# Queries of a latent attention: latent columns produced transposed, rotated columns token by token, three score banks

## The chip, the cores and the metric

One core of one Trainium2 chip runs the whole program. The metric is the device time of one execution in microseconds; lower is better.

## The reference

Four sequences of 512 tokens with 256 features go through two layers. Layer 0 is a multi-head latent attention (16 heads, causal) with a residual, and a mixture of 64 experts (6 per token) with a shared expert. Layer 1 is a Mamba-2 mixer and a ternary feed-forward network. The change touches the queries of the attention:

```python
q = rmsnorm(x @ w_qa, q_norm_w) @ w_qb          # (.., 192) @ (192, 16*(128+64))
q_nope, q_rope = q[..., :DN], q[..., DN:]       # DN = 128, DR = 64
kv = x @ w_kva                                   # (.., 64 + 64)
k_nope, v = split(rmsnorm(kv_c, kv_norm_w) @ w_kvb)
q_rope = q_rope * cos + rotate_half(q_rope) * sin
scores = einsum('blhd,bmhd->bhlm', q, k) * scale
attn = softmax(where(mask, scores, -1e30))
out = einsum('bhlm,bmhd->blhd', attn, v).reshape(B, L, H * DV) @ w_o
```

## The kernel before, in words

All data is float32. The part of w_kvb that makes the keys is folded into w_qb once, at the start (`prep_queries`), so that a head's query has 64 latent columns, matched with the normalised 64-wide latent itself, and 64 rotated columns: 128 in all (`QE`). Likewise the value part of w_kvb is folded into w_o (`prep_values`). The transposed keys `KT` hold 64 latent rows and 64 rotated rows for 512 tokens.

The attention goes by sequence (`b`, four) and in a sequence by groups of four heads (`g`, sixteen in all, numbered 0 to 15). A group has 16 slots: token tile `i = u // 4` (128 tokens) and head `h = u % 4`. For slot `u` TensorE makes the scores against `(i + 1) * 128` keys (L521) and adds the causal mask in bf16 (L522); VectorE takes the maximum (L853); ScalarE takes the exponential and its sum (L700); VectorE takes the reciprocal (L858) and normalises (L864); TensorE transposes the probabilities (L530) three slots later (`LAG`); VectorE copies them out (L873, L876); at three places of a group (slots 12, 16 and 20) TensorE multiplies them with the values (L547) and ScalarE copies these (L712). A group's last slots lie in the next group. PSUM has eight banks: four for scores in turn, two for transposed probabilities, one for values, and one (`QUERY`, bank 7) for making the next group's queries.

Compressed queries of 192 features lie transposed as `cq1` (128 rows) and `cq2` (64 rows, padded to 128 with zeros). Their products with the folded weights `wqe1`, `wqe2` (L480, L481) give four heads of one token tile: 128 tokens by 512 columns. ScalarE copies them to `qs` (L681). GpSimd rotates the 64 rotated columns of each head (`rope`, L964 to L968; VectorE does tiles 1 and 3 of a sequence's first group). TensorE turns each head's 128 x 128 (L486), and ScalarE copies the result to `QT` (L685). In a group with a successor in its sequence, products stand at slots 1, 3, 5, 7 and turns at 9, 11, 13, 15, written out by hand in tables (`PRODUCT_AT`, `TURN_AT`). Each engine runs its instructions in program order, and semaphores connect them. Between two sequences TensorE projects the next one, makes the mean squares, the output and the queries of the next sequence's first group in one piece (`first_queries`).

From the second sequence on, routing work of the sequence before stands in the slots too: logits and top-6 in a sequence's first group, ranks in its second, weights (VectorE) in its third and fourth; GpSimd scatters token rows to DRAM (L1198), eight of them among the turns made in the third group, sixteen in the fourth.

## Time and profile before

| | |
|---|---|
| three runs | 1368.81 us median, 1367.03 to 1376.04 |
| profiled execution: span from first to last instruction | 1372.1 us (no other time of that execution is given) |
| mean granted TensorE clock | 0.952 |
| busy over the span | TensorE 1236.2 us (90%), VectorE 801.9 (58%), ScalarE 463.7 (34%), GpSimd 376.6 (27%) |
| attention, first scores to last | about 59 to 642 us |

"Busy" counts time in which an engine works on at least one instruction. A TensorE matmul on float32 is recorded as two passes (so x2 for one matmul), and the recorded duration of a pass includes its way through the array; what it costs in a row of passes is the distance from start to start. PEld rows are weight loads, SPq rows DMA issues. Everything behind the attention (experts, Mamba, feed-forward) is not touched.

### The profile page before, as it was taken

Reading aid. Unit: us, or ns where it says so; the run is one execution under the profiler, and the core shown is the slowest. Engines: PE = TensorE matmul, PEld = TensorE weight load, DVE = VectorE, ACT = ScalarE, POOL = GpSimd, SP = SyncE. Lnnn points to the kernel's source line nnn. Section 1 sums busy time; section 2 is a strip of 40 time slices with the busy share of each in tenths; the row PEclk is TensorE's granted clock in tenths of the full one; section 3 lists DMA queues with packets and bytes.
Section 4 is the critical chain, followed back from the end, with each engine's and each line's share of the span. In section 5 each row is a group of like instructions: output and inputs, shape, how many; then the busy total and the mean of one; then the engine's idle time right before and its main releaser. Section 6 shows DMA issues by size and latency. Waiting matters only on the chain.

```text
span 1372.1 us, 19483 instructions
## 1 busy us (share of the span) xinstructions
PE 1236.2 (90%) x6005; PEld 767.3 (56%) x6005; DVE 801.9 (58%) x2226; ACT 463.7 (34%) x1057; POOL 376.6 (27%) x464
## 2 busy tenths in 40 slices
PE   6999999989999899988959999997585987999988
PEld 3566566555555466556536777775244545555454
DVE  6377767786578667784513434334665673685431
ACT  2455435442455335442201111111331612625310
POOL 1242023451425413351340000113564261311200
PEclk9799999999999999999979999999777998999999
DMA  9999999999800100010336888884212021000000
GB/s 320 413 419 420 420 421 420 420 420 418 334 1 32 62 1 1 8 58 30 107 103 191 274 263 269 270 278 138 67 43 62 1 70 39 12 12 16 0 16 16
DMA packets 89422, 235.48 MB, mean 172 GB/s; under 512 B 12768, under 2 KB 23680, under 8 KB 89088
## 3 DMA queue, kind: packets, MB, share of 16 engines
q1 hardware_dynamic: 70912, 192.54, 37.9%
q0 software_dynamic: 9216, 25.18, 5.8%
q10 hardware_dynamic: 9216, 16.78, 3.2%
q8 instruction: 42, 0.69, 0.2%
q14 instruction: 36, 0.29, 0.1%
HBM read 66.70 MB, written 167.77 MB: 171 GB/s over the span
## 4 chain that ended last, share of the span: by engine, by line
PE 72%; DVE 15%; issue 4%; another core or an unknown queue 3%; ACT 2%; SPq 2%; DMA 1%; POOL 1%; ACTq 0%; DVEq 0%; POOLq 0%
PE bank L521 6%; PE bank L547 5%; PE bank L480 4%; PE bank L609 4%; PE bank L530 4%; PE bank L481 4%; PE bank L1327 4%; PE bank L1349 3%; PE bank L1588 3%; PE bank L1594 3%; DVE negmax L853 3%; PE bank L1605 3%; DVE r L864 2%; PE bank L1639 2%
## 5 line engine op out<-in xcount | busy, mean ns | idle before, releaser
L700 ACT ACTIVATE r<-bank,negmax 128x128 f32<-128x128 f32 (+3 forms) x256 | 134.9, 527 | 173.7 <-DVE negmax L853 163.5
L521 PE MATMUL bank<-r 128*128 128x512 f32 (+3 forms) x512 | 184.2, 443 | 0.0
L853 DVE TENSOR_REDUCE negmax<-bank 128x1 f32<-128x128 f32 (+3 forms) x256 | 124.1, 485 | 55.9 <-PE bank L522 53.0
L530 PE MATMUL bank<-tables,r 128*128 128x128 f32 x640 | 117.7, 284 | 19.8 <-DVE r L864 18.6
L964 POOL TENSOR_TENSOR r<-r,tables 128x256 f32<-128x256 f32 x56 | 42.0, 749 | 331.7 <-ACT r L681 331.6
L1198 POOL DMA_INDIRECT sent<-r,slots x96 | 93.9, 978 | 113.0 <-ACT r L700 49.1
L530 PEld LDWEIGHTS bank<-tables,r 128*128 128x128 f32 x640 | 75.2, 145 | 74.6 <-issue 35.6
L1436 DVE COPY r<-bank 128x512 f32<-128x512 f32 x64 | 41.2, 685 | 116.3 <-PE bank L1358 75.3
L864 DVE TENSOR_SCALAR r<-r,rrow 128x128 f32<-128x128 f32 (+3 forms) x256 | 103.8, 406 | 0.3
L521 PEld LDWEIGHTS bank<-r 128*128 128x128 f32 x512 | 77.8, 191 | 23.6 <-issue 18.4
L1214 POOL DMA_INDIRECT r<-sent,slots x16 | 15.2, 950 | 223.3 <-DMA sent<-r 219.6
L480 PE MATMUL bank<-r 128*128 128x512 f32 x128 | 70.7, 634 | 3.6 <-DVE x L808 1.5
L1550 POOL TENSOR_TENSOR r<-tables,r 128x1024 f32<-128x1024 f32 x16 | 31.2, 1960 | 153.6 <-DVE r L1969 123.6
L873 DVE COPY late<-bank 128x256 f32<-128x256 f32 (+1 forms) x128 | 60.4, 472 | 16.5 <-PE bank L530 16.5
L481 PE MATMUL bank<-r 128*128 128x512 f32 x128 | 66.6, 602 | 0.0
L1394 ACT ACTIVATE r<-bank 128x512 f32<-128x512 f32 x32 | 19.1, 597 | 137.1 <-PE bank L1327 125.0
L1327 PE MATMUL bank<-r 128*128 128x256 f32 x256 | 62.4, 388 | 0.0
L1349 PE MATMUL bank<-r 128*128 128x256 f32 x256 | 61.3, 382 | 0.0
L609 PE MATMUL bank<-spent,r 128*128 128x256 f32 x256 | 57.9, 383 | 0.5 <-ACT r L712 0.5
L522 PE MATMUL bank<-futureb,identb 128*128 128x128 bf16 x256 | 56.1, 219 | 0.0
L609 PEld LDWEIGHTS bank<-spent,r 128*128 128x128 f32 x256 | 47.8, 190 | 11.8 <-issue 4.6
L1349 PEld LDWEIGHTS bank<-r 128*128 128x128 f32 x256 | 48.0, 190 | 8.9 <-issue 2.7
(276 smaller groups left out, 2404.4 us busy)
## 6 DMA issues: line engine op xcount, KB each, us to landing
sent<-gath SPq DMA_DIRECT2D x8, 16384.0 KB, 88.1
r<-waT_dram SPq DMA_DIRECT2D x64, 304.0 KB, 3.1
r<-sent SPq DMA_DIRECT2D x64, 256.0 KB
sent<-r ACTq DMA_DIRECT2D x64, 256.0 KB
w2buf<-wcT_dram SPq DMA_DIRECT2D x64, 48.0 KB, 3.5
r<-w_o_dram SPq DMA_DIRECT2D x1, 2048.0 KB, 11.2
sent<-gath SPq DMA_DIRECT2D x2, 1024.0 KB, 56.7
out_dram<-x SPq DMA_DIRECT2D x4, 512.0 KB, 2.9
```

The lines of the kernel that those rows point to most:

```text
L480: nc.tensor.matmul(bank[at][:], cq1[:, i * P:(i + 1) * P], w1, start=True, stop=False)
L481: nc.tensor.matmul(bank[at][:], cq2[:, i * P:(i + 1) * P], w2, start=False, stop=True)\
L521: nc.tensor.matmul(at[:, 0:n], QT[g % 2][:, h, i * P:(i + 1) * P], KT[:, 0:n], start=True, stop=False)
L530: last = nc.tensor.transpose(bank[TRANS[u % 2]][:, j * P:(j + 1) * P], prob[:, u % 4, j * P:(j + 1) * P], ident)
L547: last = nc.tensor.matmul(bank[VALUE][KVL * half:KVL * (half + 1), c:c + 2 * P], V[:, j, :], p[:, 2 * half:2 * half + 2, :].rearrange("p h ...
L609: last = nc.tensor.matmul(bank[4 + i % 2][:, 0:DIM], OT[:, c, i * P:(i + 1) * P], wvo[:, c, :], start=(c == 0), stop=(c == HEADS // 2 - 1))
L700: nc.scalar.activation(prob[:, u % 4, 0:(i + 1) * P], bank[SCORE[u % 4]][:, 0:(i + 1) * P], ACT.Exp, bias=negmax[:, u:u + 1], scale=1.0, a ...
L853: nc.vector.tensor_reduce(negmax[:, u:u + 1], bank[SCORE[u % 4]][:, 0:(i + 1) * P], axis=AX.X, op=ALU.max, negate=True).then_inc(A["max"], 1)
L864: nc.vector.tensor_scalar(p, p, rrow[:, u:u + 1], None, ALU.mult).then_inc(A["norm"], 1)
L1198: nc.gpsimd.indirect_dma_start(sent[:, :], bass.IndirectOffsetOnAxis(ap=slots[:, t, k:k + 1], axis=0), xn1[:, n // TOPK, :], None).then_in ...
L1327: last = nc.tensor.matmul(bank[2][:, t * ROWS:(t + 1) * ROWS], wb[:, 2 * q + t, k * EI:k * EI + EA], tokens(q, t, k), start=(k == 0), stop ...
L1349: nc.tensor.matmul(to[t][:, half * DIM:(half + 1) * DIM], hid_a[:, q % 2, c:c + P], wb[:, 2 * q + t, KC * EI:KC * EI + DIM], start=(half = ...
```

## The change

Latent columns are now produced already transposed: folded weights of two heads (128 columns) are the stationary operand and the 512 tokens of the compressed query move, so the result is `QT`'s latent rows. Only rotated columns are still made token by token, 256 instead of 512 per tile. The 64-row remainders stand twice, in rows 0 to 63 and 64 to 127, and two of them are issued one behind the other into two banks. Scores have three banks; the next group's queries have two (3 and 7).

```diff
-        wqe1, e = carve(r2, 0, (HEADS, QE))
-        wqe2, e = carve(r2, e, (HEADS, QE))
+        wl1, e = carve(r2, 0, (HEADS, KVL))
+        wl2, e = carve(r2, e, (GROUPS, P))
+        wr1, e = carve(r2, e, (HEADS, DR))
+        wr2, e = carve(r2, e, (HEADS, DR))
...
-            load(sp, "tables", wqe1[:, :, KVL:QE], a["w_qr"][0:P])
-            load(sp, "tables", wqe2[0:QL2, :, KVL:QE], a["w_qr"][P:QL])
+            load(sp, "tables", wr1, a["w_qr"][0:P])
+            load(sp, "tables", wr2[0:QL2], a["w_qr"][P:QL])
+            load(sp, "tables", wr2[QL2:P], a["w_qr"][P:QL])
...
-        VO_BANKS = (4, 5, 0, 1)
+        VO_BANKS = (0, 1, 2, 3)
...
+            pe.wait_ge(A["v"], 1)
...
-                for dst, b, n in ((wqe1, 4, P), (wqe2[0:QL2], 6, QL2)):
...
+                nc.scalar.copy(wl1[:, 8 * m:8 * m + 8, :], bank[4 + m][:].rearrange("p (h c) -> p h c", h=8))\
+                    .then_inc(prep_out, 1)
+            nc.scalar.copy(wl2, bank[6][:].rearrange("p (g c) -> p g c", g=GROUPS)).then_inc(prep_out, 1)
...
-        SCORE, TRANS, VALUE, QUERY = (0, 1, 2, 3), (4, 5), 6, 7
-        PRODUCT_AT = {1: 0, 3: 1, 5: 2, 7: 3}
-        TURN_AT = {9: 0, 11: 1, 13: 2, 15: 3}
+        SCORE, TRANS, VALUE, QUERY = (0, 1, 2), (4, 5), 6, (3, 7)
+        QSTEPS = TB + 2
+        ROPES_AT = {1: 0, 4: 1}
+        LATENTS_AT = 7
+        TURN_AT = {11: 0, 14: 1}
...
+            def rope_product(g, half, at):
+
+                heads_ = slice(g % GROUPS * HG, (g % GROUPS + 1) * HG)
+                for t in range(2):
+                    i = 2 * half + t
+                    nc.tensor.matmul(bank[at[t]][:, 0:HG * DR], cq1[:, i * P:(i + 1) * P],
+                                     wr1[:, heads_, :].rearrange("p h c -> p (h c)"), start=True, stop=False)
+                for t in range(2):
+                    i, r = 2 * half + t, slice(QL2 * t, QL2 * (t + 1))
+                    nc.tensor.matmul(bank[at[t]][:, 0:HG * DR], cq2[r, i * P:(i + 1) * P],
+                                     wr2[r, heads_, :].rearrange("p h c -> p (h c)"), start=False, stop=True)\
+                        .then_inc(A["q"], 1)
+
+            def latent_product(g, at):
+
                 hg = g % GROUPS
...
+                for p in range(2):
+                    h = hg * HG + 2 * p
+                    nc.tensor.matmul(bank[at[p]][:], wl1[:, h:h + 2, :].rearrange("p h c -> p (h c)"), cq1,
+                                     start=True, stop=False)
+                for c in range(0, SEQ, 2 * P):
+                    for p in range(2):
+                        r = slice(QL2 * p, QL2 * (p + 1))
+                        last = nc.tensor.matmul(bank[at[p]][:, c:c + 2 * P], wl2[r, hg, :], cq2[r, c:c + 2 * P],
+                                                start=False, stop=c + 2 * P == SEQ)
+                last.then_inc(A["q"], 1)
+
+            def rope_transposes(half, at):
+                for p in range(2):
+                    for t in range(2):
+                        last = nc.tensor.transpose(bank[at][:, (2 * p + t) * P:(2 * p + t + 1) * P],
+                                                   qs[:, 2 * half + t, p * P:(p + 1) * P], ident)
                 last.then_inc(A["qt"], 1)
...
             def first_queries(b):
                 g = GROUPS * b
...
+                pe.wait_ge(A["cq"], 3 * b + 3)
+                rope_product(g, 0, (6, 7))
+                rope_product(g, 1, (4, 5))
                 if b == 0:
                     prep_values(pe)
...
+                pe.wait_ge(A["qs"], QSTEPS * g + 2)
+                latent_product(g, (6, 7))
+                pe.wait_ge(A["qs"], QSTEPS * g + TB)
+                for half in range(2):
+                    turned(g, 2 * half)
+                    turned(g, 2 * half + 1)
+                    rope_transposes(half, 4 + half)
...
-                need(pe, A["exp"], NU * g + u - 3)
...
+                need(pe, A["exp"], NU * g + u - len(SCORE) + 1)
...
-            pe.wait_ge(prep_out, 8)
+            pe.wait_ge(prep_out, 3 + len(VO_BANKS))
...
+            def ql_copy(g, p, at):
+                act.wait_ge(A["q"], (TB + 1) * (g + 1))
+                for m in range(2):
+                    last = nc.scalar.copy(QT[g % 2][0:KVL, 2 * p + m, :], bank[at][KVL * m:KVL * (m + 1), :])
+                last.then_inc(A["qs"], 1)
+
+            def qt_copy(g, half, at):
+                act.wait_ge(A["qt"], 2 * g + half + 1)
+                for m in range(2):
+                    last = nc.scalar.copy(pairs(QT[g % 2])[KVL:QE, :, m, half * 2 * P:(half + 1) * 2 * P],
+                                          bank[at][DR * m:DR * (m + 1), :].rearrange("p (a l) -> p a l", a=2))
+                last.then_inc(A["qte"], 1)
 
             def first_queries(b):
...
+                g = GROUPS * b
+                for i, at in enumerate((6, 7, 4, 5)):
+                    q_copy(g, i, at)
+                for p, at in enumerate((6, 7)):
+                    ql_copy(g, p, at)
+                for half, at in enumerate((4, 5)):
+                    qt_copy(g, half, at)
                 if b == 0:
                     prep_values_out(act)
...
+                    if at in ROPES_AT:
+                        for t in range(2):
+                            q_copy(g + 1, 2 * ROPES_AT[at] + t, QUERY[t])
+                    if at - LATENTS_AT in (1, 2):
+                        ql_copy(g + 1, at - LATENTS_AT - 1, QUERY[at - LATENTS_AT - 1])
+                    if at in TURN_AT:
+                        qt_copy(g + 1, TURN_AT[at], QUERY[TURN_AT[at]])
...
+                    for r in (0, QL2):
+                        nc.vector.scalar_tensor_tensor(out=cq2[r:r + QL2, :], in0=bank[1][0:QL2, :], scalar=qn2[:],
+                                                       in1=rq[0:QL2, :], op0=ALU.mult, op1=ALU.mult)\
+                            .then_inc(A["cq"], 1)
...
-                        if b and hg == GROUPS - 1:
-                            if i == 0:
+                        if b and hg == GROUPS - 1 and i % 2:
+                            if i == 1:
                                 send_ready(pool, b - 1)
-                            send(b - 1, 2 * i)
-                            send(b - 1, 2 * i + 1)
+                            for m in range(4):
+                                send(b - 1, 2 * (i - 1) + m)
```

The order on TensorE in slots 5 to 9 of group 1, where the next group's queries are made: before, the last products (L480, L481) and the first turn (L486); L521 and L522 are scores and mask, L530 transposed probabilities.

```order
L480 MATMUL bank<-r 128x512
L481 MATMUL bank<-r 128x512
L530 MATMUL bank<-tables,r 128x128
L521 MATMUL bank<-r 128x256
L522 MATMUL bank<-futureb,identb 128x128
L530 MATMUL bank<-tables,r 128x128
L521 MATMUL bank<-r 128x256
L522 MATMUL bank<-futureb,identb 128x128
L480 MATMUL bank<-r 128x512
L481 MATMUL bank<-r 128x512
```

After, from slot 6 on (L554 and L555 are scores and mask, L563 transposed probabilities, L503 and L508 the latent columns' 128-row part and remainders):

```order
L554 MATMUL bank<-r 128x256
L555 MATMUL bank<-futureb,identb 128x128
L563 MATMUL bank<-tables,r 128x128
L554 MATMUL bank<-r 128x256
L555 MATMUL bank<-futureb,identb 128x128
L503 MATMUL bank<-r 128x512 x2
L508 MATMUL bank<-r 128x256 x4
L563 MATMUL bank<-tables,r 128x128 x2
L554 MATMUL bank<-r 128x384
```

The products of slots 5 and 7 became one block behind the scores of slot 7; the turns at slots 9, 11, 13, 15 became two, at 11 and 14.

The order on ScalarE in slots 8 to 12 of group 1: before (L700 exponentials, L685 turned queries, L712 values),

```order
L700 ACTIVATE r,rowsum<-bank,negmax 128x384 x2
L685 COPY r<-bank 128x4x128
L700 ACTIVATE r,rowsum<-bank,negmax 128x384 x2
L685 COPY r<-bank 128x4x128
L700 ACTIVATE r,rowsum<-bank,negmax 128x512
L712 COPY r<-bank 128x2x128 x2
```

and after (L749 exponentials, L724 latent pieces, L730 rotated pieces, L761 values):

```order
L749 ACTIVATE r,rowsum<-bank,negmax 128x384
L724 COPY r<-bank 64x512 x2
L749 ACTIVATE r,rowsum<-bank,negmax 128x384
L724 COPY r<-bank 64x512 x2
L749 ACTIVATE r,rowsum<-bank,negmax 128x384 x2
L730 COPY r<-bank 64x2x256 x2
L749 ACTIVATE r,rowsum<-bank,negmax 128x512
L761 COPY r<-bank 128x2x128 x2
```

Two copies became six, four of them ahead of the exponentials of slots 9 and 10.

The order on ScalarE before the first exponential of all: before (L401 folded query weights, L677 value rows, L681 and L685 queries, L407 folded values),

```order
L677 COPY r<-bank 128x256
L681 COPY r<-bank 128x512 x4
L407 COPY spent<-bank 128x512 x4
L685 COPY r<-bank 128x4x128 x4
L700 ACT_TABLE_LOAD
```

and after (L404 and L406 folded query weights, L712 value rows, L716, L724 and L730 queries, L411 folded values):

```order
L404 COPY r<-bank 128x512 x2
L406 COPY r<-bank 128x512
L712 COPY r<-bank 128x256
L716 COPY r<-bank 128x256 x4
L724 COPY r<-bank 64x512 x4
L730 COPY r<-bank 64x2x256 x4
L411 COPY spent<-bank 128x512 x4
L749 ACT_TABLE_LOAD
```

The copies of the folded values moved from ahead of the turned queries to behind them.

## Rows read from the trace of the kernel before

**Rows 1.** Groups 1, 3, 6: stretch, length, busy PE, PEld, DVE, ACT, POOL; clock; DMA.
```profile
84.10:112.30 28.20, 28.20 (x162) 17.22 (x160) 19.78 (x66) 15.52 (x45) 9.49 (x16) 1.00 1.02 420
140.50:160.00 19.50, 19.09 (x119) 11.37 (x115) 17.12 (x62) 10.67 (x35) 0.00 (x0) 1.00 1.02 419
260.60:290.20 29.60, 28.25 (x160) 16.91 (x158) 24.32 (x92) 14.85 (x44) 17.66 (x24) 1.00 1.03 420
```
**Rows 2.** The same view: third and fourth quarter of group 1, fourth of group 4.
```profile
99.60:104.60 5.00, 5.00 (x32) 3.32 (x30) 5.00 (x17) 3.26 (x10) 2.25 (x4) 1.00 1.02 419
104.60:112.30 7.70, 7.70 (x52) 4.88 (x52) 6.39 (x18) 4.80 (x13) 0.00 (x0) 1.00 1.03 422
221.10:228.70 7.60, 7.04 (x46) 4.23 (x44) 7.44 (x26) 4.31 (x12) 0.00 (x0) 1.00 1.03 421
```
**Rows 3.** Chain of waits in group 1, one product; timeline of TensorE, one turn.
```profile
85.62 0.91 PE bank L480 x2
86.54 0.86 PE bank L481 x2
...
79.00 0.61 PE L486 MATMUL bank<-tables,r 128*128 128x128 f32 x4
79.44 0.27 PE L530 MATMUL bank<-tables,r 128*128 128x128 f32 x1
```
**Rows 4.** Timeline of TensorE: start us, duration; half-height forms and their neighbours.
```profile
741.48 1.13 PE L1358 MATMUL bank<-w2buf,r 48*128 48x256 f32 x8
742.54 0.66 PE L1312 MATMUL bank<-tables,r 128*128 128x128 f32 x4
...
23.21 1.02 PE L460 MATMUL bank<-r,ones 128*128 128x512 f32 x2
24.16 1.12 PE L461 MATMUL bank<-r,ones 64*128 64x512 f32 x2
25.22 1.09 PE L346 MATMUL bank<-tables,late 128*128 128x128 f32 x8
```
**Rows 5.** Groups by form, ScalarE: busy us, mean ns | idle before, releaser.
```profile
L681 ACT COPY r<-bank 128x512 f32<-128x512 f32 x64 | 37.4, 585 | 40.6 <-PE bank L481 40.1 <-issue 0.5
L712 ACT COPY r<-bank 128x256 f32<-128x256 f32 x64 | 22.1, 372 | 38.0 <-PE bank L547 27.2 <-remote 8.9 <-issue 2.0
L664 ACT ACTIVATE r<-bank 64x512 f32<-64x512 f32 x8 | 4.7, 588 | 7.3 <-PE bank L452 7.3
```
**Rows 6.** Timeline of the start, up to the first scores.
```profile
40.83 2.03 ACT L401 COPY r<-bank 128x512 f32<-128x512 f32 x4 [3.30 <-PE bank L378]
42.95 2.04 PE L480 MATMUL bank<-r 128*128 128x512 f32 x2 [1.55 <-issue]
...
52.96 3.73 PE L393 MATMUL bank<-r 128*64 128x256 f32 x32
...
57.31 1.07 ACT L685 COPY r<-bank 128x512 f32<-128x512 f32 x2
...
58.99 0.39 PE L521 MATMUL bank<-r 128*128 128x128 f32 x2
```
**Rows 7.** Timeline: end of slot 6's exponential, scores of slot 9, group 3.
```profile
149.10 0.19 ACT L700 ACTIVATION_READ_ACCUMULATOR r<-bank,negmax 128x1 f32 x1
...
149.62 0.81 PE L521 MATMUL bank<-r 128*128 128x384 f32 x2
```
**Rows 8.** Busy time by stretch; the granted clock stands behind POOL.
```profile
991.00:996.20 5.20, 0.03 (x2) 0.01 (x1) 1.95 (x9) 4.07 (x8) 3.98 (x5) 0.83 0.36 107
996.20:1001.20 5.00, 5.00 (x24) 4.71 (x25) 3.03 (x6) 0.44 (x1) 4.17 (x3) 0.50 0.14 44
```
**Rows 9.** Timeline between the first and the second sequence.
```profile
181.93 0.73 DVE L792 SCALAR_TENSOR_TENSOR r<-bank,qn,r 64x512 f32<-64x512 f32 x1
...
184.37 0.32 PEld L472 LDWEIGHTS bank<-tables,r 64*128 64x128 f32 x4 [0.33 <-DVE r L796]
...
189.00 1.12 PE L480 MATMUL bank<-r 128*128 128x512 f32 x2 [0.52 <-DVE x L808]
...
199.16 0.39 PE L521 MATMUL bank<-r 128*128 128x128 f32 x2
```

More of the change, by code:

```diff
@@ L169, in build @@
         krope, e = carve(r2, e, (2, SEQ))
-        qs, e = carve(r2, e, (TB, HG * QE))
+        qs, e = carve(r2, e, (TB, HG * DR))
         qtmp, e = carve(r2, e, (2, HG * DR))
@@ L304, in loaded @@
             eng.wait_ge(loads[key], total_loads[key])
-        total_loads = {"first": 96, "x": 16, "tables": 48, "prep": 32, "w_o": 16, "ffn0": 80, "mamba": 112, "ffn1": 112}
+        total_loads = {"first": 96, "x": 16, "tables": 64, "prep": 32, "w_o": 16, "ffn0": 80, "mamba": 112, "ffn1": 112}
         class Norm:
@@ L484, in q_transpose @@
-            def q_transpose(i, at):
-                for h in range(HG):
-                    last = nc.tensor.transpose(bank[at][:, h * P:(h + 1) * P],
-                                               qs[:, i, h * QE:(h + 1) * QE], ident)
-                last.then_inc(A["qt"], 1)
+            def rope_product(g, half, at):
[9 more added lines that the diff above has]
+                        .then_inc(A["q"], 1)
@@ L490, in first_queries @@
             def first_queries(b):
                 g = GROUPS * b
-                if b == 0:
-                    pe.wait_ge(consts, 6)
-                pe.wait_ge(A["cq"], 2 * b + 2)
-                for i in range(TB):
-                    if i >= 2:
-                        pe.wait_ge(A["qs"], TB * g + i - 1)
-                    q_product(g, i, 7 - i % 2)
+                pe.wait_ge(A["cq"], 3 * b + 3)
+                rope_product(g, 0, (6, 7))
+                rope_product(g, 1, (4, 5))
@@ L559, in slot @@
                     pass
-                if not final and with_next and at in PRODUCT_AT:
-                    i = PRODUCT_AT[at]
-                    if i == 0:
-                        pe.wait_ge(A["qte"], TB * g + TB)
-                    else:
-                        pe.wait_ge(A["qs"], TB * (g + 1) + i)
-                    q_product(g + 1, i, QUERY)
-                if not final and with_next and at in TURN_AT:
-                    i = TURN_AT[at]
-                    pe.wait_ge(A["rope_p"], turns_before(g + 1, i) + 1)
-                    if i == 0:
-                        pe.wait_ge(A["qs"], TB * (g + 1) + TB)
-                    else:
-                        pe.wait_ge(A["qte"], TB * (g + 1) + i)
-                    q_transpose(i, QUERY)
+                if not final and with_next:
+                    if at in ROPES_AT:
+                        half = ROPES_AT[at]
+                        if half == 0:
+                            pe.wait_ge(A["qte"], 2 * (g + 1))
+                        else:
+                            pe.wait_ge(A["qs"], QSTEPS * (g + 1) + 2)
+                        rope_product(g + 1, half, QUERY)
+                    if at == LATENTS_AT:
+                        pe.wait_ge(A["qs"], QSTEPS * (g + 1) + TB)
+                        latent_product(g + 1, QUERY)
+                    if at in TURN_AT:
+                        half = TURN_AT[at]
+                        pe.wait_ge(A["qs"], QSTEPS * (g + 1) + TB + half + 1)
+                        turned(g + 1, 2 * half + 1)
+                        rope_transposes(half, QUERY[half])
+                if first and at == LAG:
+                    pe.wait_ge(A["qte"], 2 * (g + 1))
                 u = at - LAG
```

90 lines of the change are left out of this document (35 added, 55 removed).

## The prediction

> **What bounds the kernel now.** I read first the table of busy time by stretch, cut at the groups of the attention (a group: four heads of one sequence, 16 slots). In a group that also makes the next group's queries TensorE is busy throughout: 28.20 of 28.2 us, with VectorE at 19.78 and ScalarE at 15.52 [rows 1]. The last group of a sequence makes none and takes 19.5 us with TensorE at 19.09; so TensorE's work on queries sets the pace in the others, 12 of the 16 groups. Then I cut one group into quarters. In its third quarter (slots 8 to 11) VectorE is full as well, 5.00 of 5.0 us, in its fourth 6.39 of 7.7. With routing work added, VectorE has 7.44 of 7.6 us in the fourth quarter of the second sequence's first group, and 24.32 of 29.6 over its third group [rows 1, 2]. So time taken off TensorE in the first half of a group is time saved, and time taken off in the second half is saved only where VectorE is not full.
>
> **The change, part by part.**
>
> *Products in the first half.* Before, a tile's product is two matmuls of 512 columns, recorded as two passes each: 0.91 + 0.86 = 1.77 us [rows 3], four per group: 7.08 us. A pass over 512 columns is thus 0.43 us, over 256 columns 0.215. After, one half of the rotated columns is two 128-row matmuls of 256 columns (4 passes, 0.86 us) and two 64-row matmuls in the upper and the lower half of the array, into two banks. The trace has such a pair elsewhere: eight passes of 256 columns in the 48-row form, alternately from two halves of the array, run from 741.48 to the next form's start at 742.54, 1.06 us, where one after the other they would take 8 x 0.215 = 1.72 [rows 4]. So pairs run together (4 x 0.215 = 0.86), and 0.20 goes to the first load and the leaving of the form. Entering costs 0.09: the two 512-column passes before the 64-row form start at 23.21, the form at 24.16, and 0.95 - 0.86 = 0.09; the two passes in it, to 25.22, again cost 0.86 + 0.20 [rows 4]. A visit to the half-height form therefore costs 0.29 us beside its passes. Half of the rotated columns: 0.86 + 0.43 + 0.29 = 1.58; both: 3.16. The latent columns: 4 passes of 512 = 1.72, then 8 passes of 256 in pairs = 0.86 + 0.29: 2.87. Sum 6.03, with some 0.15 for the three entries behind the bf16 mask matmul (the 0.05 by which 0.91 exceeds 0.86): 6.18. Saved: 0.90 per group, 10.8 us over 12. I take 10.5.
>
> The Trainium skill, "TensorEngine Tiling (Array Packing)", Key Properties, says that changing the tiling mode drains TensorE; the row agrees that a change has a price. If each of the six changes in a group cost a drain, taken as the 0.17 by which a lone pass of 512 (0.60 recorded) outlasts its slot of 0.43, it would be 1.0 us a group instead of my 0.87: 1.6 us more in all. It neither carries nor changes the sum.
>
> *Turns in the second half.* Four 128-column transposes take 0.44 us (79.00 to 79.44) [rows 3]; a group has 16 before and 8 after: 0.88 us. What that is worth differs. In the first three groups of sequence 0, which have no routing and where VectorE leaves 1.3 us of the second half, I take 0.85 x 3 = 2.6; in the first groups of sequences 1 to 3, whose fourth quarter is full, 0.6 x 3 = 1.8; in the six others, where VectorE runs at 24.32 of 29.6, 0.15 x 6 = 0.9. Together 5.3; the ends are 0 and 12 x 0.88 = 10.6.
>
> *ScalarE.* Before, eight copies of 512 columns per group (0.585 each by the by-form row). After, four of 256 columns (0.372) and eight 64-partition pieces of 512 elements, for which the nearest row is 0.588 on 64 partitions: half the partitions save nothing [rows 5]. Two in a row take about 1.07 (57.31) [rows 6]. Four pieces now stand behind the exponentials of slots 8 and 9 and two behind that of slot 11, about 3.2 us of copies in a quarter that takes 5.0 and has ScalarE busy 3.26 in it, of which 1.1 goes. I followed the slots: the exponentials of slots 9 to 11 come 0.3, 0.9 and 1 us later than now, and VectorE's reciprocal waits for them; TensorE then has some 1.5 us of value products at slot 12, which hold up the scores of slot 13 anyway, and behind them the lateness ends; ScalarE has 4.80 of 7.7 us to do in that quarter. I cost it at nothing because of that cover; without it it is 1 to 2 us a group (the third rival).
>
> *Three score banks.* Scores of slot u now wait for the exponential of u-3, not u-4. In the tightest stretch of before, slots 8 to 12 of a last group, the scores of slot 9 start at 149.62, while the exponential three slots back has its accumulator read at 149.10 for 0.19, thus ends at 149.29: 0.33 us to spare [rows 7]. Transposes of u-3 already wait for a later step of the same chain. Cost 0; queued behind such a wait would be the query products and everything on TensorE, and VectorE would wait for those.
>
> *Start.* ScalarE's four copies of folded weights take 2.03 us and release the first product at 42.95; three take 1.5: -0.5 us. Cold products: 2 x 3.0 us at half clock, to 48.5. Then value folding, 3.7 [rows 6], to about 52.5, and the latent columns to 55.5, the transposes to 56.4. Now ScalarE: it stood idle for the folded values before, and copied them while they were made; after, its order is four query copies, four latent pieces, four rotated pieces and only then four copies of folded values. From 55.6: 2.1 + 2.1 + 2.1 us, so the first scores, which wait for all of them, start at about 62.0 instead of 58.99 [rows 6]: +3.0. TensorE stands idle for some 5.5 us then. In the trace a stretch of 5.2 us with TensorE busy for 0.03 is followed by 5.0 us at a granted clock of 0.50, the 1.2 GHz level [rows 8]; slots 0 to 3 would run some 3.7 us of work partly at that level: +1.8 (between 0 and 2.5). The Trainium skill, "TensorE: Matmul & The Clock Gate", HAM oscillation, says idle gaps throw the clock back; the trace agrees.
>
> *Between sequences, three times.* VectorE writes the remainder of the compressed query twice, one more 0.73 us (181.93) ahead of the key latents, for which TensorE already waits 0.33 us [rows 9]: with back-to-back overlap of 0.07 and slack of 0.3, +0.33. From the first product at 189.00 to the first scores at 199.16 it is 10.2 us. After: products and latents done at +6.1, ScalarE's latent pieces at +8.4 and rotated pieces at +9.5 and +10.6: -0.4 in effect, as the exponentials queue behind the last. TensorE's work now has idle time of some 2 us in front of the first scores and again until the first exponential; between no loss of clock and 2 us of it, I take 0.8. Sum +0.7 x 3 = 2.1.
>
> *Loads, sends.* The rotated weights arrive in rows of 4 KB rather than in pieces, so SyncE's queue moves on sooner; nothing waits for them but work behind 41 us. GpSimd's sends stand in fours behind two turns, and the turn for slot 14 is due many us later. Zero for both.
>
> **Sum.** -10.5 - 5.3 + 3.0 + 1.8 + 2.1 = -8.9 us. It is made against the profiled execution, whose span is 1372.1; the three runs have a median of 1368.8 and no launch time of the profiled one is given, so the difference is carried over: 1368.8 - 8.9 = 1360 us. The likeliest case alone spans 1353 to 1367.
>
> **Rivals.**
> - *All TensorE time is saved.* The last group's 19.5 us with VectorE at 17.12 speaks for it; the full quarters against. 12 x 1.75 = 21, less 3.0 at the start, no clock losses: 1351.
> - *VectorE or ScalarE takes the whole second half.* Then only the first half counts: -10.5 + 6.9 = -3.6: 1365.
> - *ScalarE's pieces hold up the exponentials, slower than before.* If both pairs behind slots 8 and 9 are exposed, 2.1 us x 12 = 25 us are added and the second half's gain is gone: -10.5 + 25 + 6.9 = +21.4: 1390. It makes the kernel slower by over 1% from 1.4 us a group on ((13.7 + 10.5 - 6.9)/12). For it: VectorE is full in that quarter, so nothing lost there comes back in it. Against it: the value products at slot 12.
> - *The half-height pairs run one after the other*, so that the change doesn't do what it says: 1.72 us x 12 = 20.6 more: +11.7, 1380. The pairs elsewhere [rows 4] speak against it.
>
> **How the numbers follow.** Forecast 0.48, all saved 0.20, second half lost 0.17, ScalarE exposed 0.10, no pairing 0.05. About 1% (13.7 us) is what a measurement tells from no change: faster means under 1355.1. Faster: 0.20 + 0.12 of the forecast's own range = 0.32. Slower, above 1382.5: 0.10 and 0.03 of the rest. The same: 0.55. The range 1347 to 1378 leaves out the third rival, most of the fourth, and the edge of the first.
>
> **What would show it.** Right: first halves of groups shorter by 0.9 us, second halves by 0.9 in sequence 0 and by little with routing; half-height passes in pairs a few ns apart; the first maximum near 62.5 us, with the clock at half behind it; no wait of scores on exponentials of over 0.2 us a slot. Wrong: reciprocals waiting on exponentials in slots 9 to 11 by more than 1.4 us a group; quarters three and four shorter together by over 1.5 us; half-height passes 0.2 us apart.

## The result, and the profile after

The changed kernel takes 1372.27 us (median of 14 runs, 1369.97 to 1379.49) beside 1368.61 for the kernel before (14 runs): ratio 1.0038, 95% interval 1.002 to 1.0057: slower by 0.4%, clear of noise. The forecast was 1360. Its profiled execution has a span of 1371.4 us and a mean granted clock of 0.951 (before: 1372.1 and 0.952).

The spans hide the comparison, since what follows the attention varies by some us from profile to profile (741 to 747 on this chip, whatever the kernel), and the profile of the kernel before lies above its median: elsewhere a time is 1.8 us more than its span, which would make it some 1374 us (an estimate) beside 1368.61. So I compare the attention alone, up to the last maximum of a score row: it starts at 627.4 us before, at 629.7 after. Busy time by stretch, groups 1, 3 and 6, the third and the fourth quarter of group 1, then the gap and the stretch behind it at the start and at the second sequence (columns as in [rows 1]):

```profile
89.18:116.20 27.02, 26.84 (x168) 16.63 (x164) 20.87 (x65) 16.57 (x48) 9.18 (x16) 1.00 1.02 420
143.20:162.14 18.94, 18.47 (x113) 10.95 (x109) 16.90 (x60) 10.29 (x34) 0.00 (x0) 1.00 1.02 420
262.54:291.97 29.43, 27.20 (x164) 16.17 (x162) 24.17 (x92) 16.56 (x48) 17.44 (x24) 1.00 1.02 419
103.70:109.40 5.70, 5.70 (x38) 3.60 (x38) 5.03 (x17) 5.01 (x13) 0.00 (x0) 1.00 1.03 420
109.40:116.20 6.80, 6.80 (x48) 4.16 (x44) 6.39 (x18) 5.64 (x14) 0.00 (x0) 1.00 1.02 420
56.60:62.50 5.90, 0.00 (x0) 0.00 (x0) 0.00 (x0) 5.75 (x12) 0.00 (x0) 0.94 1.02 422
62.50:69.30 6.80, 6.79 (x25) 4.92 (x26) 2.37 (x12) 3.63 (x11) 1.72 (x4) 0.55 1.03 425
200.50:202.00 1.50, 0.00 (x1) 0.02 (x1) 0.00 (x0) 1.44 (x4) 0.00 (x0) 0.92 1.02 421
202.00:205.00 3.00, 2.99 (x10) 2.31 (x10) 0.79 (x4) 2.96 (x7) 0.00 (x0) 0.50 1.02 422
```

Against [rows 1], group 1 is down from 28.20 to 27.02 and group 6 from 29.6 to 29.4. Quarters three and four of group 1 are 5.7 and 6.8 beside 5.0 and 7.7 [rows 2]: ScalarE's pieces lengthen one, and the later one gives it back (the run with small pieces, below, shows both). The last four rows are the losses: TensorE idle for 5.9 us at the start and for 1.5 us between sequences, with ScalarE at work in both, and half clock (1.2 of 2.4 GHz) behind each. Another 1.1 us of idle time stands before those 1.5 (198.73 to 199.87 us), where TensorE waits for the columns that VectorE rotates; the kernel before has gaps of 0.33 and 0.49 us in this stretch. Before, no such fall came at any of the three later sequence starts.

Timeline of the start and of the second sequence's first queries:

```profile
55.62 2.37 ACT L724 COPY r<-bank 64x512 f32<-64x512 f32 x4 [6.00 <-PE bank L508]
58.02 2.37 ACT L730 COPY r<-bank 64x512 f32<-64x512 f32 x4
60.41 2.05 ACT L411 COPY spent<-bank 128x512 f32<-128x512 f32 x4
62.51 0.79 PE L554 MATMUL bank<-r 128*128 128x128 f32 x2 [5.91 <-ACT spent L411]
...
184.09 1.51 DVE L846 SCALAR_TENSOR_TENSOR r<-bank,qn,r 64x512 f32<-64x512 f32 x2
...
187.08 0.46 PE L481 MATMUL bank<-tables,r 64*128 64x64 f32 x4 [0.49 <-DVE r L850]
...
191.71 1.13 PE L490 MATMUL bank<-r 128*128 128x256 f32 x4 [0.52 <-DVE x L862]
...
198.19 2.37 ACT L724 COPY r<-bank 64x512 f32<-64x512 f32 x4 [2.35 <-PE bank L508]
...
200.59 2.37 ACT L730 COPY r<-bank 64x512 f32<-64x512 f32 x4
202.01 0.77 PE L554 MATMUL bank<-r 128*128 128x128 f32 x2 [1.51 <-ACT r L730]
```

ScalarE's order is the forecast's, and its latent pieces begin at 55.62 as forecast; but four pieces take 2.37 us, 0.59 each, not 2.1. First product to first scores between sequences is now 10.30 us (10.16 in [rows 9]), and from there to the first maximum it is 0.98 us at half clock instead of 0.55.

TensorE's timeline in group 1, a rotated half and then the latent columns, each with what follows it:

```profile
89.87 1.08 PE L490 MATMUL bank<-r 128*128 128x256 f32 x4
90.88 0.70 PE L494 MATMUL bank<-r 64*128 64x256 f32 x4
91.52 0.66 PE L563 MATMUL bank<-tables,r 128*128 128x128 f32 x4
...
99.59 1.94 PE L503 MATMUL bank<-r 128*128 128x512 f32 x4
101.46 1.14 PE L508 MATMUL bank<-r 64*128 64x256 f32 x8
102.52 0.44 PE L563 MATMUL bank<-tables,r 128*128 128x128 f32 x2
```

A half takes 1.65 us from start to next start (forecast 1.58) and the latents 2.93 (2.87). In the single passes the two products of a pair start 6 to 7 ns apart; entering the half-height form costs about 0.09 us, leaving it 0.10, the first pair 0.10, and the second pass behind it comes 0.05 us late. With that, a group's products are 2 x 1.70 + 2.98 = 6.38 us instead of 7.08.

The distance from one group's first maximum to the next (from single records), in us after minus before: the first maximum of all +3.98; group 0 +1.07; groups 1 and 2 -1.18 each; groups 4, 8, 12 (first of a sequence) -0.72, +0.23, +0.37; groups 5, 9, 13 -0.6 each and 6, 10, 14 -0.2 each; groups 3, 7, 11 with the boundary behind them +0.60, +1.27, +0.64; group 15 -0.3. Sum +2.3.

### The profile page after: what moved, and what is told of

Its sections match the earlier page's. It is cut to its first block, busy times and chain, and to the rows that moved or that the text cites. A ratio compares the mean times of both kernels' runs of the same rounds, so it can differ in the third digit from the quotient of the medians.

```text
span 1371.4 us, 19610 instructions
## 1 busy us (share of the span) xinstructions
PE 1215.1 (89%) x6069; PEld 763.0 (56%) x6069; DVE 815.4 (59%) x2230; ACT 485.6 (35%) x1120; POOL 374.1 (27%) x462
## 4 chain that ended last, share of the span: by engine, by line
PE 56%; DVE 20%; SPq 10%; issue 8%; ACT 2%; another core or an unknown queue 2%; DMA 1%; POOL 1%; DVEq 0%; ACTq 0%; POOLq 0%
PE bank L554 7%; PE bank L580 4%; PE bank L563 4%; PE bank L1640 3%; PE bank L1646 3%; DVE negmax L907 3%; PE bank L644 3%; DVE r L918 3%; PE bank L1657 3%; SPq L1336 2%; PE bank L490 2%; SPq L1328 2%; PE bank L1801 2%; PE bank L1691 2%
## 5 line engine op out<-in xcount | busy, mean ns | idle before, releaser
L554 PE MATMUL bank<-r 128*128 128x512 f32 (+3 forms) x512 | 187.1, 449 | 10.3 <-ACT spent L411 5.9
L749 ACT ACTIVATE r<-bank,negmax 128x128 f32<-128x128 f32 (+3 forms) x256 | 135.0, 528 | 163.8 <-DVE negmax L907 156.8
L563 PE MATMUL bank<-tables,r 128*128 128x128 f32 x640 | 121.2, 290 | 32.2 <-DVE r L918 30.9
L563 PEld LDWEIGHTS bank<-tables,r 128*128 128x128 f32 x640 | 72.1, 145 | 93.6 <-DVE r L918 59.8
L1488 DVE COPY r<-bank 128x512 f32<-128x512 f32 x64 | 41.2, 686 | 115.7 <-PE bank L1410 74.5
L918 DVE TENSOR_SCALAR r<-r,rrow 128x128 f32<-128x128 f32 (+3 forms) x256 | 109.6, 428 | 0.3
L554 PEld LDWEIGHTS bank<-r 128*128 128x128 f32 x512 | 80.2, 197 | 29.3 <-issue 18.1
L644 PE MATMUL bank<-spent,r 128*128 128x256 f32 x256 | 57.9, 383 | 0.5 <-ACT r L761 0.5
L555 PE MATMUL bank<-futureb,identb 128*128 128x128 bf16 x256 | 56.7, 221 | 0.0
L1480 DVE COPY r<-bank 128x512 f32<-128x512 f32 x64 | 41.2, 682 | 20.1 <-PE bank L1364 18.4
L580 PE MATMUL bank<-late,r 128*64 128x256 f32 x384 | 52.0, 409 | 0.0
```

Source lines behind the costliest of these rows:

```text
L554: nc.tensor.matmul(at[:, 0:n], QT[g % 2][:, h, i * P:(i + 1) * P], KT[:, 0:n], start=True, stop=False)
L555: nc.tensor.matmul(at[:, i * P:n], identb[:], futureb[:], start=False, stop=True)\
L563: last = nc.tensor.transpose(bank[TRANS[u % 2]][:, j * P:(j + 1) * P], prob[:, u % 4, j * P:(j + 1) * P], ident)
L580: last = nc.tensor.matmul(bank[VALUE][KVL * half:KVL * (half + 1), c:c + 2 * P], V[:, j, :], p[:, 2 * half:2 * half + 2, :].rearrange("p h ...
L644: last = nc.tensor.matmul(bank[4 + i % 2][:, 0:DIM], OT[:, c, i * P:(i + 1) * P], wvo[:, c, :], start=(c == 0), stop=(c == HEADS // 2 - 1))
L749: nc.scalar.activation(prob[:, u % 4, 0:(i + 1) * P], score_bank(g, u)[:, 0:(i + 1) * P], ACT.Exp, bias=negmax[:, u:u + 1], scale=1.0, acc ...
```

## The experiments

Ratios are to the kernel before, measured beside each on the same chip. The first four ran on a chip where it takes 1368.07 us, the next four on one where it takes 1319.45, the last four on a third, 1318.94. The groups whose clock doesn't fall have the same length on all three, except the last ones of the later sequences, so lengths are compared across chips and totals only within one chip. The edits are shown shortened.

**Folded values ahead of the pieces.**

```
 q_copy x4
+if b == 0: prep_values_out(act)
 ql_copy x2; qt_copy x2
-if b == 0: prep_values_out(act)
```

> Changed kernel, with the four copies of the folded values put back ahead of the latent pieces on ScalarE at the start. Theory A (the start lost its time to this order, and the clock fell because TensorE stood idle for 5.9 us): first maximum at about 61.4 us instead of 63.52 (the four copies took 2.05), group 0 shorter by 0 to 1.5 us as less of it runs at 1.2 GHz; in all -2 to -3.5 us, ratio to the kernel before about 1.001 to 1.002. Rival (the start is bound by something else, the loss lies in the groups): first maximum later than 62.8, ratio unchanged at 1.0038.

Measured: 1367.78, ratio 0.9997 (0.9974 to 1.002). The first maximum came at 60.37 instead of 63.52. Timeline of its start:

```profile
52.56 0.58 ACT L411 COPY spent<-bank 128x512 f32<-128x512 f32 x1 [0.28 <-PE bank L397]
...
55.55 2.37 ACT L724 COPY r<-bank 64x512 f32<-64x512 f32 x4 [2.40 <-PE bank L508]
57.94 2.36 ACT L730 COPY r<-bank 64x512 f32<-64x512 f32 x4
59.39 0.76 PE L554 MATMUL bank<-r 128*128 128x128 f32 x2 [2.87 <-ACT r L730]
```

The folded values hide in ScalarE's idle time again, and 3.15 us of the start's loss is their place in the order. That is 1.1 more than their own 2.05: the first scores no longer wait for anything behind the first two rotated pieces. Group 0 stayed at 25.7: TensorE's gap was 2.87 us instead of 5.91, and the clock still fell.

**The second half in slot 3.**

```
-ROPES_AT = {1: 0, 4: 1}
+ROPES_AT = {1: 0, 3: 1}
```

> Changed kernel, with the second half of the rotated columns made at slot 3 instead of 4. Theory C (the product moved out of the first quarter, where VectorE now sets the pace in the groups with routing, into the second, where TensorE does): quarters 1 and 2 together of groups 5, 6, 9, 10, 13, 14 shorter by 0.4 to 0.9 us each, those of groups 1 and 2 unchanged within 0.1; in all -3 to -6 us, ratio about 1.000. Rival (the place does not matter, the first half is as long as its work): no quarter sum moves by over 0.15 us, ratio 1.0038.

Measured: 1372.74, ratio 1.0043 (1.0021 to 1.0065). Group 1:

```profile
88.37:114.99 26.62, 26.62 (x168) 16.62 (x164) 21.22 (x66) 16.54 (x48) 9.15 (x16) 1.00 1.02 420
```

TensorE is busy for all of its 26.62 us: 1.58 under before, which is the products' 0.70 and the turns' 0.88 to the hundredth. So 0.40 us of the changed kernel's 27.02 is a wait made by the slot. Theory C had expected nothing here. The wait is one for VectorE: with no product in slots 2 and 3 of the changed kernel, a transpose is due before its row is normalised. Group 1 of the changed kernel, then TensorE's transposes on the whole page, before and after:

```profile
92.82 0.48 DVE L918 TENSOR_SCALAR r<-r,rrow 128x128 f32<-128x128 f32 x1
93.35 0.14 PEld L563 LDWEIGHTS bank<-tables,r 128*128 128x128 f32 x1 [0.40 <-DVE r L918]
```
```profile
L530 PE MATMUL bank<-tables,r 128*128 128x128 f32 x640 | 117.7, 284 | 19.8 <-DVE r L864 18.6
```
```profile
L563 PE MATMUL bank<-tables,r 128*128 128x128 f32 x640 | 121.2, 290 | 32.2 <-DVE r L918 30.9
```

Little of these 12 us more is the wait of groups 1 and 2: in this run, which is rid of it, the same row still has 30.4. The rest stands where VectorE sets the pace and TensorE, with less to do, waits longer.

Groups 5, 9, 13 gained 0.4 too, 6 and 14 nothing to 0.1, so Theory C's place for the gain was half right. The first groups of sequences 1 to 3 were 0.5 to 1.1 us longer, why was not looked into, and group 10 was 1.2 us longer with a fall of the clock at 415.9 (the runs with folded values first and with small pieces have one there too). Together that took it all back.

**Three score banks alone, in the kernel before.**

```
-SCORE = (0, 1, 2, 3)
+SCORE = (0, 1, 2)
```

> The kernel before with three score banks instead of four and nothing else. My theory: no cost, group lengths within 0.1 us of before, ratio 1.000. Rival D (three banks make TensorE wait for exponentials): the last groups of the sequences and the third quarters get longer by 0.2 us or more each, 2 us or more in all, ratio 1.0015 or above.

Measured: 1368.52, ratio 1.001 (0.9985 to 1.0036), all groups within 0.03 us of before but 7, 11 and 15, which are 0.2 to 0.4 shorter. Giving up the fourth score bank costs nothing there.

**Latent pieces of 16 columns.** This leaves out most of the latent query columns.

```
-copy(QT[..., :], bank[...][..., :])
+copy(QT[..., 0:16], bank[...][..., 0:16])
```

> Changed kernel, in which each latent piece that ScalarE copies is 16 columns wide instead of 512, so that most latent columns of the queries are left out of the result. Theory B (ScalarE's pieces hold up the exponentials in the third quarter and the first scores between sequences): third quarter of groups 1 and 2 at 4.6 to 5.0 us instead of 5.69, first maximum of the sequences earlier by 1.5 to 2.3 us each, group 1 at 26.3 instead of 27.02; in all -10 us or more. Rival (TensorE and VectorE set the third quarter): it stays above 5.4 us, and only the four starts shorten.

Measured: 1366.39, ratio 0.9969 (0.994 to 0.9999). The third quarter of group 1 fell to 4.82 us, as Theory B had it, and VectorE is full in it again:

```profile
101.48:106.30 4.82, 4.82 (x30) 3.01 (x30) 4.82 (x17) 3.16 (x13) 0.00 (x0) 1.00 1.03 420
```

But the fourth quarter grew by as much, from 6.81 to 7.68, and groups 1 and 2 didn't move: 27.02. Group 3 with its boundary fell to 57.77 (changed kernel 59.77), the last score came at 621.1 instead of 629.7. ScalarE between the first and the second sequence:

```profile
195.97 0.72 ACT L724 COPY r<-bank 64x16 f32<-64x16 f32 x4 [2.35 <-PE bank L508]
196.72 1.17 ACT L730 COPY r<-bank 64x512 f32<-64x512 f32 x2
```

So the pieces hold up the exponentials and cost nothing all the same inside groups, since TensorE is busy throughout; they cost about 2 us at every sequence start (1.6 at the first maximum, 2.0 to 2.5 at the others), where nothing covers them.

**VectorE takes one latent bank of the first queries**, behind its turns.

```
 # VectorE, first_ropes
+for m in range(2): nc.vector.tensor_copy(QT[..][.., 2 + m, :], bank[7][..])
 # ScalarE
-ql_copy(g, 0, 6); ql_copy(g, 1, 7)
+ql_copy(g, 0, 6)
```

> The changed kernel with one of the two latent banks of a sequence's first queries copied out by VectorE, behind its two turns, instead of by ScalarE (two of the eight 64x512 pieces move). Theory A (ScalarE's row of 64-partition pieces, 0.59 us each, sets when a sequence's first scores start, and the idle TensorE behind it lets the clock fall): the distance from the first product block to the first scores at 191.7 falls from 10.3 to about 9.5 us, TensorE's gap there from 1.51 to about 0.7 us, and the granted clock no longer falls at 201.8, 358.8 and 515.8; each boundary 1.2 to 2 us shorter, the first scores of the program 1.2 us earlier (61.3 instead of 62.5); time 4 to 6 us below the changed kernel, 1366.5 to 1368.5. Theory B (VectorE is as late as ScalarE there, since its turns end at 199.7): no boundary moves by more than 0.3 us, only the start gains; time 1371.

Measured: 1314.92, ratio 0.9966 (0.9954 to 0.9979). Group 3 with its boundary 58.58, first groups at 27.20 without a fall of the clock, and the gap of 1.5 us halved:

```profile
198.85 0.46 PE L554 MATMUL bank<-r 128*128 128x128 f32 x2 [0.75 <-DVE r L861]
```

The chain of waits in front of the first scores of the second sequence now goes through VectorE:

```profile
196.43 0.91 DVE r L1026
197.34 0.02 issue
197.36 0.68 DVE r L861
198.05 0.01 issue
198.06 0.70 DVE r L861
198.76 0.09 issue
198.85 0.46 PE bank L554 x2
```

Theory A holds for ScalarE and the starts; but the falls didn't vanish, they moved to 255.9, 406.0 and 556.2, where groups 6, 10 and 14 took 30.4 us instead of 29.4. TensorE has a gap of 1.22 us just before 255.9; the changed kernel has the same one, 1.23 us, at 258.5 and no fall behind it.

**All three edits together**: folded values first, VectorE's copies, slot 3 outside a sequence's first group.

> The changed kernel with three edits: the folded values are copied out ahead of the latent pieces at the start, VectorE copies one of the two latent banks of the first queries, and the second rotated half stands in slot 3 instead of 4, except while a sequence's first group runs. If the three losses found so far (start 3.2 us, boundaries 0.8 us and the clock's fall, 0.4 us in the groups whose slot 3 holds the half) are apart and add up: first maximum at 60.0 or a little before, groups 1 and 2 at 26.62, group 0 at 25.7 as in the changed kernel, boundaries 1.2 to 2 us shorter, and the last score 8 to 11 us ahead of the changed kernel's 629.7; time 1361 to 1364, below both kernels. If something else takes over (a router's chain, the stream of expert rows behind the attention), the last score is early and the rest of the program is longer by as much: time 1367 to 1369.

Measured: 1308.04, ratio 0.9915 (0.9899 to 0.9931): faster than both kernels, and the gains roughly add. First maximum 57.9, groups 1 and 2 26.62, last score 604.0 (616.4 in the changed kernel, unchanged, on the third chip). TensorE's gap at the start is 1.64 us, and the clock did not fall behind it: group 0 took 23.84 us, where 25.7 was expected. It still fell for 3.4 us at 193.8, 344.0 and 494.1, and the first groups there took 28.8 us. In front of 193.8 stand gaps of 1.15 and 0.75 us, the same as with VectorE's help alone, where no fall came at this place: the length of the gap by itself does not decide.

**The remainders not side by side.**

```
-i, r = 2 * half + t, slice(QL2 * t, QL2 * (t + 1))
+i, r = 2 * half + t, slice(0, QL2)
```

> The changed kernel with both rotated remainders of a block read from rows 0 to 63 instead of one from 0 to 63 and one from 64 to 127. Theory A (two 64-row products in different halves of the array run at the same time, as the 6 ns between their starts say): each rotated half costs 0.43 us more (two more passes of 256 columns at 0.11 each for either tile), so groups 1 and 2 are at 27.5 to 27.9 instead of 27.02, and the last score is 6 to 13 us later. Theory B (the starts are only recorded together and the array takes them one after the other anyway): no group moves by more than 0.1 us.

Measured: 1335.93, one run, so I read lengths of groups and not the total (0.8 us in each of twelve groups would be 10 of its 16; its clock also stands at half for longer at the start). Groups 1 and 2 took 27.84, 0.83 more than the changed kernel's.

```profile
97.31 1.13 PE L494 MATMUL bank<-r 64*128 64x256 f32 x4
98.37 0.66 PE L563 MATMUL bank<-tables,r 128*128 128x128 f32 x4
```

1.06 us instead of 0.64 for the same four passes: pairing saves 0.42 a half, the 0.43 that the forecast's fourth rival would have lost.

**The gap filled**: ten transposes into an unused bank behind the last turns of each later sequence's first queries.

```
+if b:
+    for n in range(10):
+        nc.tensor.transpose(bank[0][:, 0:P], qs[:, 0, 0:P], ident)
```

> The changed kernel with ten more 128x128 transposes into an unused bank behind the last transposes of the first queries of sequences 1 to 3, where TensorE otherwise waits 1.5 us for ScalarE's pieces. Theory A (that idle time is what makes the granted clock fall to 0.5 for 3.4 us at each of the three starts): no fall at 201.8, 358.8 and 515.8, the first scores at the same time, groups 4, 8 and 12 shorter by up to 1.7 us each, time 2 to 5 us below the changed kernel (1367.5 to 1370.5). Theory B (the clock falls because of the weak stretch before it, some 12 us of output products and waits): it falls all the same, time 1372.

Measured: 1314.1, ratio 0.996 (0.9943 to 0.9977). TensorE does more work, and from 65.9 to 615.4 us the clock never fell. The first groups of sequences 1 to 3, this kernel, then the changed kernel unchanged and the kernel before, both on the third chip:

```profile
201.52:229.00 27.48, 26.45 (x164) 17.06 (x161) 21.14 (x77) 18.57 (x51) 9.15 (x16) 1.00 1.02 420
351.62:379.10 27.48, 26.45 (x164) 17.06 (x161) 21.14 (x77) 18.58 (x51) 9.15 (x16) 1.00 0.69 282
501.57:529.05 27.48, 26.45 (x164) 17.05 (x161) 21.13 (x77) 18.58 (x51) 9.15 (x16) 1.00 0.00 1
```
```profile
200.96:230.85 29.89, 29.00 (x164) 18.68 (x163) 20.91 (x78) 18.36 (x50) 9.25 (x16) 0.91 1.02 420
353.77:382.22 28.45, 27.55 (x164) 17.88 (x163) 20.81 (x77) 18.39 (x51) 9.16 (x16) 0.96 0.58 236
505.05:534.57 29.52, 28.63 (x164) 18.53 (x163) 20.72 (x77) 18.34 (x50) 9.46 (x16) 0.92 0.00 1
```
```profile
198.18:227.21 29.03, 28.33 (x160) 17.63 (x157) 20.96 (x77) 16.66 (x46) 9.39 (x16) 1.00 1.03 420
```

The clock alone costs 2.4 + 1.0 + 2.0 = 5.4 us there; without it the first groups are 1.5, 1.2 and 1.2 us shorter than before. Without this idle time the fall does not come, which is Theory A; the gap of 1.1 us before it stayed, and the weak stretch that Theory B named was left as it was.

**Both kernels unchanged on the third chip.**

> The kernel before, unchanged, profiled on the same chip as the kernels beside it, since the last four ran on a chip where it takes 1319 us instead of 1369. If the changed kernel's balance there is the one read so far, this profile has groups 1 and 2 at 28.20 us, first maximum at 59.5, and its sequence boundaries and the stretch behind the last score show what that chip does differently.

> The changed kernel, unchanged, on the same chip as the others of this call. If its balance is a matter of the kernel alone, its ratio to the kernel before is again 1.002 to 1.006. If on another chip a different wait ends the boundaries (there the groups 7 and 11 with the stretch behind them took 61.2 us instead of 64 to 66), the ratio can differ by 0.005 either way.

Measured: the changed kernel 1319.47 (12 runs), ratio 1.0001 (0.9991 to 1.0011). The balance has the first chip's pattern: start +3.92, group 0 +0.66, groups 1 and 2 -1.19, boundaries +0.58, +1.06, +1.09, last score +3.87; groups 4 and 12 are 0.8 longer than before, since two of the falls last 6.8 us here and not 3.4. On the first chip groups 7 and 11 take 4 to 5 us more and the rest behind the last score some 40 us more, in either kernel; why was not looked into (in group 7 1.9 us of it stand in the second quarter, 7.03 beside 5.12, at full clock). The profile of before has no fall of the clock from 46.1 us to 694.6, and at 1316.31 us it lies below its median of 1318.94: the medians differ less than the two profiles, and where the changed kernel gets the 3.9 us back in the median is not shown.

**All three edits and six filling transposes.**

> The kernel with all three edits (folded values copied first, VectorE copying one latent bank of the first queries, the second rotated half in slot 3 outside a sequence's first group), and six more 128x128 transposes into an unused bank behind the last transposes of the first queries of sequences 1 to 3, in the 0.75 us that TensorE waits there. Theory A (the granted clock falls at these starts only because TensorE idles): no fall at 193.8, 344.0 and 494.1, groups 4, 8 and 12 at 27.2 instead of 28.8, last score about 599 instead of 604.0, time some 5 us below the kernel with the three edits, ratio to the kernel before 0.987 to 0.989. Theory B (where the fall comes depends on other stretches too): a fall stays somewhere, and the ratio is 0.990 to 0.992 as without the filling.

Measured: 1303.57, ratio 0.9887 (0.9869 to 0.9904). No fall between 47 and 682 us, last score 599.2. The second sequence's first group:

```profile
193.47:220.67 27.20, 26.32 (x164) 17.12 (x163) 20.99 (x77) 18.26 (x50) 9.16 (x16) 1.00 1.02 420
```

**One write of the remainder.** For sequences 1 to 3 VectorE writes rows 0 to 63 alone (and TensorE waits for one write less), so part of their query columns comes from sequence 0.

```
-for r in (0, QL2):
+for r in ((0, QL2) if b == 0 else (0,)):
```

> The changed kernel with the remainder of the latents written to rows 0 to 63 alone for sequences 1 to 3 (rows 64 to 127 keep sequence 0's, so that part of the query columns is computed from the wrong sequence). Theory A (the second write costs the boundary what TensorE waits longer there, 0.49 instead of 0.33 us): each of the three boundaries is 0.1 to 0.3 us shorter, 0.3 to 0.9 us in all, which the total can't show. Theory B (it delays VectorE's residuals and with them the first queries by its own length): each boundary is 0.75 us shorter, 2.2 us in all.

Measured: 1319.22, ratio 1.0002 (0.9991 to 1.0012). The boundaries are 0.53, 0.50 and 0.90 us shorter than in the changed kernel: between the theories, nearer to the write's whole length of 0.75 than to the 0.16 of TensorE's longer wait.

## Why the prediction was wrong

The forecast's -8.9 us became +2.3 in the attention of the first chip, 11.2 us off.

- *Groups: -15.8 forecast (10.5 for the products, 5.3 for the turns), about -9.6 measured at full clock* (-0.75 for group 0 in the kernel with the three edits, -2.4 for 1 and 2, -4.0 for 4, 8, 12 with the gap filled, -2.4 for the six others). This is the largest miss, and the step that failed is the premise that time taken off TensorE in the first half of a group is time saved, in full and in all twelve groups, because TensorE was busy there [rows 1]. Cut at VectorE's maxima, the first halves are shorter by 6.9 us together and not by 10.5, the second halves by 2.7 and not by 5.3. The sizes on TensorE were nearly right: products 6.38 us against 6.18, the turns' 0.88 exact. What failed is what they are worth:
  - The four products stood in slots 1, 3, 5 and 7; the two halves at 1 and 4 leave slots 2 and 3 without any, and TensorE waits for the normalisation: 0.40 us in groups 1 and 2, and another 0.4 each in groups 5, 9 and 13. With the halves at 1 and 3, groups 1 and 2 gain all of the 1.58, so the big block at slot 7 costs them nothing.
  - The six later groups gave 2.4 of 6.2. In 6, 10 and 14 the other slot gives 0.0 to 0.1 on the third chip. Their second half was VectorE's before the change and is after it (fourth figure of the rows below, 15.70 of 15.87 us, then 15.58 of 15.75), so turns taken off TensorE there are worth next to nothing, as the forecast's small term for them assumed. The first half of group 6, where TensorE was full, shrank by 0.1 all the same; in 10 and 14 it gave 0.4, of which the second half took back 0.2. What holds these was not settled. The halves of group 6 before, then after, third chip:

```profile
259.06:272.79 13.73, 13.73 (x69) 7.98 (x68) 8.65 (x33) 6.86 (x22) 10.08 (x15) 1.00 1.02 418
272.79:288.66 15.87, 14.51 (x93) 8.94 (x91) 15.70 (x59) 8.00 (x22) 7.58 (x10) 1.00 1.03 420
```
```profile
262.08:275.73 13.65, 13.39 (x82) 8.27 (x81) 8.56 (x32) 5.79 (x22) 9.94 (x15) 1.00 1.02 418
275.73:291.48 15.75, 13.80 (x84) 7.90 (x82) 15.58 (x60) 10.74 (x26) 7.46 (x10) 1.00 1.03 420
```

- *Start: +3.0 forecast, +3.98 measured* to the first maximum. Cause and place are right, and the reordering gives 3.15 back. The size missed by the pieces: "two in a row take about 1.07" made four 2.1, where they take 2.37 (twice 0.27). The other 0.45 is the first scores, which run at half clock: 1.01 us to the maximum instead of 0.56.
- *Clock at the start: +1.8 forecast, +1.8 measured* (25.66 against 23.84 for group 0 in the kernel with the three edits, where it did not fall).
- *Boundaries: +0.7 each forecast, 0.8 of it for the clock.* This is the second step that failed. The term for the second write, +0.33 from a wait, measures 0.5 to 0.9; that all VectorE has left in its queue moves with the write is my reading of that; "-0.4" for the shorter product row is +0.14, because ScalarE's 4.7 us row of pieces, not TensorE, now sets the first scores; and the first scores themselves run at half clock, 0.98 us to the maximum instead of 0.55. That is 1.1 us (0.5, 0.14 and 0.43), from which a shorter first quarter of the last group takes 0.5 in group 3 only. The three together measure +2.5 against the -0.2 forecast without the clock; 1.3 of it is the half clock under the first scores.
- *Clock at the boundaries: +0.8 each forecast;* in the groups behind them it is +3.9 us together on the first chip (groups 4, 8, 12 against 27.48) and +5.4 on the third. The forecast knew of idle time but let two idle spells of 2 us share one small price.
- *Three banks, ScalarE's pieces inside the groups, pairs of half-height products:* all as forecast, at 0, 0 and 0.42 us a half; the rivals built on their opposites fall. "Second half lost" is partly true: cut at the maxima, the second half of group 1 is 0.24 us shorter, not 0.85, and just as much with pieces of 16 columns, so the pieces are not why. The first half is 0.94 shorter, and in the run with the other slot the two make up the whole 1.58.
- *Signs:* the first maximum with half clock behind it and the pairs 6 to 7 ns apart came as written, and first halves 0.9 shorter in groups 1 and 2; in groups 5, 9 and 13 it was 0.35, and second halves in sequence 0 gave 0.0 to 0.24 and not 0.9.

What the forecast lacked is one view. It read which engine is full inside the groups and priced what the change takes off it. At the sequence starts no group's work covers anything, and there the change hands TensorE's and VectorE's short chain to ScalarE's long one; and inside the groups it read which engine is full, and not what a block between two slots covers. Sum of the terms: groups +6.2, start +1.0, clock +1.5, boundaries +2.7, group 15 -0.3: 11.1 of the 11.2.

With the three edits and the filling the idea is worth what was forecast and more: 0.9887 of before, some 15 us, on a chip where the changed kernel alone stands at 1.0001.

## What to carry to other kernels

A saving on the busiest engine counts in full only where its other work still covers the short chains of the other engines: here moving one block by one slot was worth 0.40 us of a group's 1.58, while making one block of the last two cost nothing. Price the places where the pipeline starts apart from its steady state; an edit that trades one engine's time for many small copies on another is paid there in full, and each idle spell may be paid twice, by a clock that falls behind it (here 3.9 to 5.4 us over three starts). Where such a gap can't be closed, harmless work in it can be worth more than it costs, as the ten transposes were.

## What was not expected of the hardware

- A copy of 64 partitions by 512 elements takes ScalarE 0.59 us, like one of 128 partitions, and four in a row take 2.37, so nothing of one hides in the next. The four copies of 128 by 512 right behind them take 2.05 (60.41), 0.51 each, as the pair in [rows 6] did. Which property of the pieces makes the difference was not tried.
- Moving work can move the falls of the clock instead of ending them: with VectorE's help they left the sequence starts (201.8, 358.8 and 515.8 in the changed kernel on the first chip) for 255.9, 406.0 and 556.2 (second chip), behind a gap of 1.22 us that the changed kernel has too, without a fall. Gaps of 1.15 and 0.75 us had a fall behind them with all three edits and none with one, and a gap of 1.64 us at the start had none. What decides was not found. The Trainium skill, "TensorE: Matmul & The Clock Gate", HAM oscillation, describes the clock falling back behind recurring waits for DMA, longer than these. The traces agree that idle time brings falls on, since filling 1.1 of the 1.5 us ended them, and show it for gaps this short, with falls of 3.4 or 6.8 us at the 1.2 GHz level.
- Two products in the upper and lower half of the array run side by side with starts 6 to 7 ns apart; one visit to the half-height form costs some 0.3 us beside its passes.
